# Four transformer blocks on one core: VectorE's SBUF copies and products as scalar_tensor_tensor, under new tables of order

## The reference

```
layer 0   h = rmsnorm(x) * (1 + scale) + shift ; attention with one head of 256 ; x += ; again with the MLP
layer 1   h = ln(x) * (1 + s) + b ; 16 heads of 16, q and k divided by their norms ; gated x += ; MLP, gated
layer 2   h = ln(x) * g + be, scaled and shifted ; 16 heads of 16, softmax(q k / 4) ; gated x += ; MLP, gated
layer 3   w-conditioned ln ; 16 heads of 16 ; x += ; last w-conditioned ln is the output
```

## Time and profile before

| what | us |
| --- | --- |
| median of 3 runs (lowest, highest) | 1109.22 (1108.21, 1112.39) |
| profiled execution, whole | 1107.05 |
| its span, first to last instruction | 1105.3 |
| TensorE busy | 1055.9 |
| VectorE busy | 833.9 |
| ScalarE busy | 709.0 |
| GpSimd busy | 503.5 |

### The profile page before, as it was taken

How to read it: one execution, slowest core, us unless ns; L and a number is a source line. 1 busy time by engine, 2 the same in 40 slices (tenths; PEclk the granted TensorE clock), 3 DMA queues, 4 the chain that set the end, 5 groups by cost and what they waited for, 6 DMA issues and landing times.

```text
span 1105.3 us, 19686 instructions
## 1 busy us (share of the span) xinstructions
PE 1055.9 (96%) x6705; PEld 689.8 (62%) x6705; DVE 833.9 (75%) x1663; ACT 709.0 (64%) x1181; POOL 503.5 (46%) x447
## 2 busy tenths in 40 slices
PE   7999999999989989999999999999999999999986
PEld 4878887755656656666566566566566576545443
DVE  7676669776586685456977977977977968998983
ACT  2453534396676676676666676677667666686764
POOL 2474753615545545544355454355344452721442
PEclk9999999999989999999999999999999999999999
DMA  7010001320502402332032131031121222232301
GB/s 245 20 39 20 11 10 29 78 61 27 149 2 77 106 6 62 88 86 50 11 100 74 50 94 46 21 106 40 26 72 31 47 51 54 58 78 57 98 11 40
DMA packets 36386, 64.46 MB, mean 58 GB/s; under 512 B 7208, under 2 KB 22312, under 8 KB 36288
## 3 DMA queue, kind: packets, MB, share of 16 engines
q1 hardware_dynamic: 36288, 63.20, 21.4%
HBM read 22.90 MB, written 2.12 MB: 23 GB/s over the span
## 4 chain that ended last, share of the span: by engine, by line
PE 70%; DVE 16%; issue 5%; POOL 3%; ACT 3%; DMA 1%; SPq 1%; DVEq 0%; POOLq 0%; ACTq 0%
PE rings L630 13%; PE rings L632 11%; PE rings L631 11%; PE rings L747 11%; PE rings L732 10%; DVE m L1278 4%; PE rings L707 4%; PE rings L786 2%; PE rings L676 2%; POOL gT_l L1384 2%; PE rings L791 1%; PE rings L657 1%; PE rings L803 1%; DVE gT_h L1259 1%; DVE m L1254 1%
## 5 line engine op out<-in xcount | busy, mean ns | idle before, releaser
L941 ACT ACTIVATE probs<-rings 128x512 f32<-128x512 f32 x572 | 302.7, 607 | 120.0 <-PE rings L707 67.0
L1278 DVE TENSOR_REDUCE m<-rings 128x1 fp32r<-128x512 f32 x512 | 316.3, 678 | 12.3 <-PE rings L707 10.1
L732 PE MATMUL rings<-SQ,SK 64*128 64x512 f32 x768 | 234.4, 441 | 9.7 <-DVE modb L1063 2.8
L732 PEld LDWEIGHTS rings<-SQ,SK 64*128 64x128 f32 x768 | 108.5, 185 | 150.1 <-issue 62.3
L747 PE MATMUL rings<-probs,V 128*32 128x512 f32 x1536 | 196.5, 607 | 0.0
L707 PE MATMUL rings<-SK,SQ 63*128 63x512 f32 x512 | 189.1, 450 | 1.1 <-ACT probs L941 0.6
L1384 POOL TENSOR_TENSOR gT_l<-gT_f,gT_h 128x512 fp32r<-128x512 f32 x96 | 129.8, 1375 | 111.7 <-DVE gT_h L1259 111.7
L1259 DVE CAST gT_h<-gT_f 128x512 fp32r<-128x512 f32 x96 | 82.5, 888 | 57.3 <-ACT gT_f L1003 56.0
L630 PE MATMUL rings<-w_h,gT_h 128*128 128x256 f32 x384 | 112.9, 294 | 6.3 <-POOL gT_l L1384 3.3
L938 ACT ACTIVATE probs<-rings 128x1024 f32<-128x1024 f32 x98 | 96.3, 1034 | 24.5 <-issue 12.0
L631 PE MATMUL rings<-w_l,gT_h 128*128 128x256 f32 x384 | 107.5, 280 | 0.0
(11 more groups left out here) (202 smaller groups left out, 2083.3 us busy)
## 6 DMA issues: line engine op xcount, KB each, us to landing
SQ<-qh SPq DMA_DIRECT2D x96, 128.0 KB, 2.6
SK<-kh SPq DMA_DIRECT2D x96, 128.0 KB, 2.7
SQ<-ql SPq DMA_DIRECT2D x48, 128.0 KB, 2.6
...
```

Source lines behind the costliest of these rows:

```text
L732: mm = pe.matmul(o[:, :], SK[a % 4][r:r + KS + 1, n // 2, c * P:(c + 1) * P], SQ[a % 4][r:r + KS + 1, n // 2, :], start=True, stop=True)
L941: act.activation(probs[:, n % PROBS, :], bank(kind, a, i)[:, :], ACT.Exp, scale=SCALE[layer(unit_job(a))]).then_inc(done["scores"], 1)
L1278: nc.vector.tensor_reduce(m16[:, col:col + 1], bank(kind, a, i)[:, :], AX_X, ALU.max, negate=True).then_inc(done["max"], 1)
```

## The change

Two things change together.

1. Instructions. `tensor_copy` of a float32 SBUF tensor to its rounded form (L1067, L1259) becomes scalar_tensor_tensor: (full * 1) max full. `tensor_scalar` and `tensor_tensor` on SBUF operands in norm2, mod, qkroot, qknorm and kbar become scalar_tensor_tensor of the same values. In mod the addition of 1 goes into the two products, which takes one instruction and its `link` away, and a second `link`. Not changed: the first copies of the program (L1070, L1075), norm1 of layer 0 (L1148), soft0 (L1298), the integer steps of qkroot, and every operation that reads PSUM.
2. Order. Every table of numbers and every pattern is new, and START too. Two waits on ScalarE keep the shared tile `sq` (also `mrow`) from being overwritten, since its two users may now follow one another the other way round.

The core of the diff (the tables are represented by FFN, which is used for layers 1 and 2):

```diff
-FFN = {"hT2": (23.77, 23.78), "fc1": (24.07, 24.63, 24.66, 24.92, 28.07, 28.09, 28.15, 28.3), "gelu": (24.95, 29.13),
-       "fc2a": (26.1, 27.16), "fc2": (31.26, 32.12)}
...
+FFN = {"hT2": (24.17, 24.19), "fc1": (25.44, 25.49, 25.65, 25.91, 29.08, 29.61, 29.73, 29.79), "gelu": (25.61, 29.36),
+       "fc2a": (27.95, 28.44), "fc2": (31.36, 33.3)}
...
+SQ_READ, _read_sq = {}, None
+for _s in PLAN:
+    if _s[0] == "modrow" or _s[0] == "qkss" and _s[2] == 0:
+        SQ_READ[_s] = _read_sq
+    if _s[0] in ("mod", "qkss"):
+        _read_sq = _s
...
+                    if SQ_READ[(kind, a, i)] and SQ_READ[(kind, a, i)][0] == "qkss":
+                        act.wait_ge(done["qkss"], NTH[SQ_READ[(kind, a, i)]])
...
+                    if i == 0 and SQ_READ[(kind, a, i)][0] == "mod":
+                        act.wait_ge(pe_ring, USE[SQ_READ[(kind, a, i)]] + 1)
...
-                    if l < LAYERS - 1:
-                        link(nc.vector.tensor_scalar(sc, sc, 1.0, None, ALU.add))
-                    link(nc.vector.tensor_tensor(mods[:, q, n:n + 2, :], sc, g, ALU.mult))
-                    link(nc.vector.tensor_tensor(sc, sc, be, ALU.mult))
-                    nc.vector.tensor_tensor(modb[:, q, n:n + 2, :], sc, sh, ALU.add).then_inc(done["mod"], 1)
+                    one = 1.0 if l < LAYERS - 1 else 0.0
+                    nc.vector.scalar_tensor_tensor(out=mods[:, q, n:n + 2, :], in0=sc, scalar=one, in1=g, op0=ALU.add, op1=ALU.mult)
+                    link(nc.vector.scalar_tensor_tensor(out=sc, in0=sc, scalar=one, in1=be, op0=ALU.add, op1=ALU.mult))
+                    nc.vector.scalar_tensor_tensor(out=modb[:, q, n:n + 2, :], in0=sc, scalar=1.0, in1=sh, op0=ALU.mult,
+                                                   op1=ALU.add).then_inc(done["mod"], 1)
...
-                    nc.vector.tensor_copy(hi, full).then_inc(rounded[kind], 1)
+                    nc.vector.scalar_tensor_tensor(out=hi, in0=full, scalar=1.0, in1=full, op0=ALU.mult, op1=ALU.max
+                                                   ).then_inc(rounded[kind], 1)
...
-                            ins = nc.vector.tensor_scalar(tok2[:, t, :], X[:, TT * b + t, :], rstd[:, 1, t:t + 1],
-                                                          None, ALU.mult)
+                            ins = nc.vector.scalar_tensor_tensor(out=tok2[:, t, :], in0=X[:, TT * b + t, :], scalar=1.0,
+                                                                 in1=rstd[:, 1, t:t + 1].to_broadcast([P, DIM]),
+                                                                 op0=ALU.mult, op1=ALU.mult)
...
-                            ins = nc.vector.tensor_scalar(tok2[:, t, :], X[:, TT * b + t, :], mv[:, 1, t, 0:1],
-                                                          rstd[:, 1, t:t + 1], ALU.subtract, ALU.mult)
+                            ins = nc.vector.scalar_tensor_tensor(out=tok2[:, t, :], in0=X[:, TT * b + t, :],
+                                                                 scalar=mv[:, 1, t, 0:1],
+                                                                 in1=rstd[:, 1, t:t + 1].to_broadcast([P, DIM]),
+                                                                 op0=ALU.subtract, op1=ALU.mult)
...
-                        link(nc.vector.tensor_tensor(root[:, :, :], rs[:, :, :], rs[:, :, :], ALU.mult))
+                        link(nc.vector.scalar_tensor_tensor(out=root[:, :, :], in0=rs[:, :, :], scalar=1.0, in1=rs[:, :, :],
+                                                            op0=ALU.mult, op1=ALU.mult))
...
-                    nc.vector.tensor_tensor(v, v, r, ALU.mult).then_inc(done[kind], 1)
+                    nc.vector.scalar_tensor_tensor(out=v, in0=v, scalar=1.0, in1=r, op0=ALU.mult, op1=ALU.mult
+                                                   ).then_inc(done[kind], 1)
...
-                            nc.vector.tensor_tensor(kbar[:, i, :].rearrange("p (n k) -> p n k", n=4),
-                                                    total.unsqueeze(1).to_broadcast([P, 4, P]),
-                                                    of_head.unsqueeze(2).to_broadcast([P, 4, P]), ALU.mult).then_inc(kbar_ready, 1)
+                            nc.vector.scalar_tensor_tensor(out=kbar[:, i, :].rearrange("p (n k) -> p n k", n=4),
+                                                           in0=total.unsqueeze(1).to_broadcast([P, 4, P]), scalar=1.0,
+                                                           in1=of_head.unsqueeze(2).to_broadcast([P, 4, P]),
+                                                           op0=ALU.mult, op1=ALU.mult).then_inc(kbar_ready, 1)
...
-                        nc.vector.tensor_copy(gT_h[:, m, :], gT_f[:, m, :]).then_inc(g_hi, 1)
+                        nc.vector.scalar_tensor_tensor(out=gT_h[:, m, :], in0=gT_f[:, m, :], scalar=1.0, in1=gT_f[:, m, :],
+                                                       op0=ALU.mult, op1=ALU.max).then_inc(g_hi, 1)
```

More of the change, by code:

```diff
@@ L73 @@
[L73 to L82, removed]
[3 rows of a table removed]
[L86 to L105, removed]
-FFN = {"hT2": (23.77, 23.78), "fc1": (24.07, 24.63, 24.66, 24.92, 28.07, 28.09, 28.15, 28.3), "gelu": (24.95, 29.13),
-       "fc2a": (26.1, 27.16), "fc2": (31.26, 32.12)}
-FFN3 = {"hT2": (18.25, 18.75), "fc1": (24.59, 25.0, 25.13, 25.36, 28.97, 29.13, 29.47, 30.55), "gelu": (25.29, 30.3),
-        "fc2a": (27.13, 27.61), "fc2": (31.04, 32.18)}
@@ new lines @@
+FFN0 = {"hT2": (14.74, 16.07), "fc1": (18.48, 19.92, 20.1, 20.18, 20.49, 23.75, 25.32, 29.26), "gelu": (18.54, 28.22),
+        "fc2a": (27.47, 28.21), "fc2": (33.68, 36.98)}
+FFN2 = {"hT2": (16.15, 17.91), "fc1": (23.46, 23.49, 23.78, 24.32, 28.33, 29.28, 30.57, 31.11),
+        "gelu": (24.73, 30.46), "fc2a": (28.46, 29.2), "fc2": (33.28, 33.79)}
+FIRST = {("merge", 0, 0): -59.79, ("mergerow", 0, 0): -58.61, ("v", 0, 0): -57.23, ("v", 0, 1): -45.73,
+         ("modrow", 0, 1): -167.74, ("headscale", 1, 0): -113.71, ("mod", 0, 1): -57.47, ("split_wp", 0, 0): -123.42,
[3 rows of a table added]
@@ new lines @@
+NEXT1 = {("modrow", 1, 0): -27.24, ("mod", 1, 0): -2.96, ("load_mod", 1, 1): -15.5, ("modrow", 1, 1): 0.47,
+         ("mod", 1, 1): 41.75, ("load_gate", 1, 0): 6.81, ("split_qkv", 1, 0): 41.74, ("load_qkv", 1, 1): 37.01,
+         ("split_qkv", 1, 1): 45.69, ("load_qkv", 1, 2): 38.6, ("split_qkv", 1, 2): 56.17, ("load_qkv", 1, 0): 9.98,
+         ("vones", 4, 0): 56.38, ("vones", 5, 0): 65.23}
+LEAD_IN = {"stat1": (-24.36,), "norm1": (-22.94,), "hT1": (-20.47, -20.06), "qktok": (-13.31, -13.09, -12.29, -11.44),
+           "qkss": (-12.33, -11.57, -11.37, -11.05), "qkroot": (-11.0,), "v": (-7.04, 0.03),
+           "qknorm": (-10.89, -10.54, -10.51, -10.26), "q": (-8.61, -7.71), "k": (-8.83, -8.74),
+           "stack": (-21.38, -4.0, -2.19, 1.98),
+           "gmax": (-7.12, -6.5, -6.38, -5.65, -5.1, -4.91, -4.85, -4.85, -4.85, -4.62, -4.2, -3.87, -3.48, -3.31, -3.31, -3.28),
+           "shift1": (-2.42, -1.78), "crow": (-21.23, -17.67, -8.94, -4.54)}
@@ new lines @@
+FFN1 = {"hT2": (14.09, 16.49), "fc1": (18.71, 21.13, 23.77, 24.8, 27.17, 27.3, 29.38, 31.89), "gelu": (21.85, 29.17),
+        "fc2a": (28.22, 31.42), "fc2": (32.91, 33.8)}
+START = [("load_mod", 0, 0), ("stat1", 0, 0), ("split_qkv", 0, 0), ("load_w1", 0, 0), ("load_qkv", 0, 0),
+         ("load_qkv", 0, 2), ("modrow", 0, 0), ("norm1", 0, 0), ("mod", 0, 0), ("load_qkv", 0, 1),
+         ("split_qkv", 0, 2), ("load_w1", 0, 2), ("load_mod", 0, 1), ("hT1", 0, 0), ("load_wp", 0, 0),
+         ("load_mod", 1, 0), ("load_w1", 0, 3), ("hT1", 0, 1), ("split_qkv", 0, 1), ("stat1", 1, 0), ("q", 0, 0),
+         ("load_rows", 0, 0), ("load_w2", 0, 0), ("q", 0, 1), ("k", 0, 0), ("load_w1", 0, 1), ("k", 0, 1),
+         ("norm1", 1, 0)]
```

90 lines of the change are left out of this document (50 added, 40 removed), and 9 rows, old and new, of tables (FIRST, SINGLE0).

## The result

| | before | after |
| --- | --- | --- |
| median (lowest, highest), us | 1111.07 (1108.21, 1113.64), 10 runs | 1116.01 (1113.38, 1121.27), 10 runs |
| ratio to before, 95% interval | | 1.0048 [1.0029, 1.0067] |
| span of the profiled execution | 1105.3 | 1114.5 |
| TensorE, VectorE, GpSimd busy | 1055.9, 833.9, 503.5 | 1067.3, 855.3, 530.0 |

The changed kernel is 5 us slower, 0.5%; 1101 was forecast, 8 us faster.

A forecast was written before the change was run, and what follows sets the result against it. TensorE was taken as the bound, with VectorE's pace counting for 16% of the span. VectorE -11, GpSimd +2.4 and order 0 gave -8.6: 1098.5 from 1107.05, so 1101 for the runs; range 1086 to 1129.

The forecast's parts named there:

- Does the new form wait? ... I take no wait.: VectorE's rewritten operations beside GpSimd: the new form never waits, so VectorE loses 29.9 us of work.
- The rows chosen for "no wait": Trace rows of L1173 (481 ns) and L1211 (292 ns), taken as nearest evidence that the new form does not wait.
- The rival "waits as the old one did": VectorE's new form waits behind GpSimd as the copy did: 1126 us, range 1118 to 1135; chance 0.30.
- The prediction's own signs of being wrong: In the profile after: gT_h mean above 1.1 us, single ones near 1.8 us, VectorE near 880 us.
- The base price: VectorE's rounding step without any wait: 749 ns as scalar_tensor_tensor against 408 for the copy, 0.34 us more.
- the rival's +49 us for VectorE: The waiting rival's VectorE total: 48.3 us for rounding steps, some 5 for other forms, less 4.6 for mod.
- 34 us more, up to 67: GpSimd's operations held by the longer rounding steps: 34 us more on 503.5, 67 at most.
- That the new tables would cover it on the way to `fc2a`: `fc2a` stands farther behind GELU, 1.15 to 2.34 ticks, so other TensorE work covers the wait for gT_l.
- Its price at the end, 0.07 us for each: GpSimd's chain share over busy share, 3% / 46%: its added time moves the end by 2.4 us, 4.7 at most.
- What a VectorE microsecond is worth: Each VectorE microsecond saved moves the end by 0.21 to 0.38; 29.9 us give 6.4 to 11.4, taken as 11.
- I count the order as zero: The new places of steps in the tables neither save nor cost anything, with 8 us to either side.
- The 57.3 us of the earlier trace: TensorE's waits for row maxima before the change, 101 times; the order's bound of 8 us is a seventh of them.

The follow-up runs named there:

- m2: Small separate programs, not the kernel: pairs of one VectorE and one GpSimd operation on 128x512, ScalarE starting the second; alone, scalar_tensor_tensor 692 ns, copy 427.
- e3: The kernel before with only the 142 rounding steps rewritten as scalar_tensor_tensor, old order: 1138.72 us, ratio 1.0253.
- e4: The changed kernel with its 142 rounding steps as copies again, other new instructions and new order kept: 1093.18 us, ratio 0.9841.
- e1: All new instructions under before's tables, without the two ScalarE waits: 1139.38 us, ratio 1.0259.
- e12: Kernel before with the 142 rounding steps as tensor_reduce (1097.85 us), plus an unused 0.28 us reduction before each: 1106.44 us, ratio 0.9976.
- e2: Before's instructions under after's tables, with the two ScalarE waits: 1094.71 us, ratio 0.9857.

## Why the prediction was wrong

*"Does the new form wait? ... I take no wait."* This step failed, and it decided the sign. The runs showed in its place that it waits as the copy did: in after 55 of the 96 gT_h steps start inside a GpSimd operation and take 1600 ns in the mean, the other 41 take 688. The rows chosen for "no wait" were not of the case. Of the four L1173 in the earlier trace rows the first came before GpSimd and held it (the row gives them together: four of 0.48 us from 1099.30 on). The last two did start inside L1394 and did not wait, 479 and 480 ns, but that GpSimd operation works on 128x4, beside which no full wait shows; gT_h mostly meets GpSimd's operations on 128x512. L1211 in the earlier trace rows started 0.2 us after GpSimd had ended. The row that did speak was the tensor_tensor L1210, 1.40 us for 0.29 of work, and the rule of the Trainium skill that the prediction cites gave the same. The rival "waits as the old one did" had the mechanism, 63 us of waits before and 55 after. The prediction's own signs of being wrong came: a mean of gT_h above 1.1 us and single ones near 1.8 (VectorE came to 855 us, not 880).

*The base price.* 749 ns was taken from L1244, which reads PSUM and a column (why it takes that is not known: with an operand in PSUM the form took 692 in m2). Two SBUF tensors take 0.69 us in this kernel, 0.27 more than the copy, not 0.34. And in the old order a step that waits grew by less than one that doesn't: the gT_h steps that start inside a GpSimd operation have a mean of 1145 ns before (62 of them) and 1304 in e3 (65). Under the new tables both grew alike, from 1324 to 1600 (55 each in e4 and after). So the rival's +49 us for VectorE measured +27.0 in e1, and +21.4 in after.

*GpSimd.* 34 us more, up to 67, were worked out from the earlier trace rows; +26.5 was measured. That term was right in its mechanism and near in its size. That the new tables would cover it on the way to `fc2a` was right too: TensorE's weight loads wait 1.3 us for gT_l in after, 12.3 in e1. Its price at the end, 0.07 us for each, was not tested alone.

*What a VectorE microsecond is worth.* 0.21 to 0.38 was right for run time of steps that conflict with nobody: e12 says 0.38. For steps that do conflict, and beyond what the copies cost, the end moved by 0.8 to 1.1 us for each microsecond that VectorE was busier, with GpSimd's part in it. A share of the chain prices an engine at its present length; that it fails once a stretch gets longer than its cover is how I read this, and no run tests it by itself. In after such a stretch is the one shown at 650 us: 5.12 us of rounding, with maxima and mod queued behind.

*Order.* "I count the order as zero" with 8 us to either side. It was 16 us (e2), twice the bound. The 57.3 us of the earlier trace rows were the wrong base for it: waits for maxima fell by 10, and TensorE's busy time rose by 8 in a stretch that was not read at all, the layer 1 jobs from 200 to 400 us with TensorE busy 186 of 200.

*Sum.* Forecast: -11 for VectorE, +2.4 for GpSimd, 0 for order. Measured: +21 for the instructions, -16 for the order. That the measured 1116 lies inside the range from 1086 to 1129 is luck: two missed terms cancel in good part, and none of the cases held. The waiting rival alone said 1126, with a price per step too high, a price per microsecond too low, and no order.

Not settled: why added time is so much dearer once the steps conflict (0.8 to 1.1 against 0.38), how much of that goes through GpSimd and how much through TensorE's clock, and which entries of the tables carry the 16 us.
